# Fused cross-attention and FFN layer on one core: the attention's ACT, POOL and SP programs written out over all heads and rows instead of looped

## The chip, the cores and the metric

The kernel runs on one core of a Trainium2 chip. The metric is device time in microseconds (us), of which the median over several executions is given. The core has TensorE (PE), VectorE (DVE), ScalarE (ACT), GpSimd (POOL) and the DMA-issuing SyncE (SP), each with its own instruction stream; they meet only at semaphores.

## What is computed

A cross-attention layer followed by a feed-forward layer, over x of 4 x 512 tokens of width 512 (2048 rows) and a context of 4 x 1601 rows (6404 keys for every token, 16 heads of width 32). Cut to the attention:

```python
q = (x @ Wq + bq).reshape(1, B * N, H, hd)
kv = (cond @ Wkv + bkv).reshape(1, -1, 2, H, hd)
q = _fq_sym(q * scale, axis=-1); k = _fq_sym(k, axis=-1); v = _fq_sym(v, axis=2)
attn = einsum('bhqd,bhkd->bhqk', q, k)
attn = softmax(attn, axis=-1)
attn = _fq_unsigned(attn, axis=-1)      # round to 0..255 steps of the row's maximum
out = einsum('bhqk,bhkd->bhqd', attn, v)
x = x + out @ Wp + bp                   # then the FFN: LN, W1, gelu, W2, with block quantisation
```

## The kernel before

The program runs in phases, each ended by a barrier: weights of the FFN, queries, keys and values, the attention, and the rest (`finish`). The attention (lines 618 to 975) is the long one, from about 650 to 2590 us.

It works on 256 **rows**: a row is one head with one tile of 128 tokens; 16 token tiles (QT) make a head, and 16 heads follow each other. For a row:

- PE (`row_of_scores`, line 732) multiplies the tile's queries with all 6404 keys, in five chunks of about 1281 columns, into two alternating PSUM buffers `ps_s`.
- DVE (line 784) copies each chunk to the row buffer `s_row` in `arena` and takes its maximum; semaphore `scores_taken`.
- POOL joins the five maxima (lines 884, 891, 896) and makes the bias of the exponent (line 901); `bias_ready`.
- ACT (line 836) takes the exponent in two halves, which it writes as bytes (`n8`) and as int16 (`n16`), both in `arena`; `exp_done[0]` and `exp_done[1]`.
- SP transposes both halves by DMA: lines 711 (bytes, two to a word, into `words_T`) and 717 (into `nT`).
- POOL unpacks the bytes into `nT` (lines 909 and 910); `unpacked`.
- PE multiplies `nT` with the head's values (line 745) three rows later (LAG = 3), in four parts between the chunks of that later row, and ACT takes the output (line 842).

`s_row`, `nT` and the others hold two rows. So DVE can't write row n+2 before the exponent of row n has read `s_row`, and PE, whose program is in order, holds the next scores back when the values' part in front of them waits for `unpacked`. Within each head, ACT issues the loads for the next head: keys and queries (lines 808 and 810) at its token tiles 2 to 4, values (lines 815 to 820) at 5 to 7. POOL scales and rounds the next head's values (lines 922 and 930) at tiles 8 to 13.

How the programs are written: PE is looped in part, and has 16 written-out heads with a loop over the last 12 rows of each. DVE is written out over all 256 rows. ACT is written out for heads 0, 1, 14 and 15, and runs heads 2 to 13 in a loop whose body is two heads. POOL is written out for head 0, runs heads 1 to 14 in a loop of two heads with a loop over eight rows in each, and head 15 in a loop of two rows. SP runs all rows but the first two in a loop of two rows. In a loop the value that a wait compares with depends on the loop's counter, and is computed into a register. `settle` raises a semaphore that nobody waits for, by one, between two waits.

Of the kernel before, what the change touches and what calls it, by code (L numbers as in the profile page):

```python
# [42 lines left out]
def settle(eng, sem):  # L43


    eng.sem_inc(sem, 1)
# [573 lines left out]
def attention(nc, A, arena, q_dram, k_dram, v_dram, scales, v_scale, attn, zinv, wp, vectors, wp_loaded):  # L620

    T, K, C, H, HD = A.T, A.K, A.C, A.H, A.HD
    QT = T // P
# [4 lines left out]
    PAIRS = ROWS // 2  # L628
# [32 lines left out]
    VP = 3  # L661
# [3 lines left out]
    with Phase(nc, "a") as ph:  # L665
# [28 lines left out]
        sp_passed = ph.sem("sp_passed")  # L694
        pool_passed = ph.sem("pool_passed")
# [7 lines left out]
        @block.sync  # L703
        def _(sp):
            def turn(pair, u):
                row = pair * 2 + u
                after_first(sp, unpacked, row - 1)
                settle(sp, sp_passed)
                sp.wait_ge(exp_done[0], row + 1)
                settle(sp, sp_passed)  # L710
                sp.dma_start_transpose(words_T[:, u, :].rearrange("p (t q) -> p t q", q=P),
                                       n8[:, u, :].bitcast(U16)).then_inc(turned[u][0], 16)
                after_first(sp, values_done, row - 1)
                settle(sp, sp_passed)
                sp.wait_ge(exp_done[1], row + 1)
                settle(sp, sp_passed)
                sp.dma_start_transpose(nT[:, u, HALF_TILES:KT], n16[:, u, :].bitcast(FP16)).then_inc(turned[u][1], 16)

            turn(0, 0)
            turn(0, 1)  # L720
            with sp.Fori(1, PAIRS) as pair:
                for u in range(2):
                    turn(pair, u)

        @block.tensor
        def _(pe):
# [29 lines left out]

            PP = QT // 2

# [44 lines left out]
        def _(act):  # L803
# [41 lines left out]
            def rows_of_head(h, slot, last=False):  # L845
                for t in range(QT):
                    row = h * QT + t
                    exponent(row, t % 2)
                    if not (isinstance(row, int) and row < TAKE_LAG):
                        take_output(row - TAKE_LAG, t % 2)  # L850
                    if not last and 2 <= t < 8 and not (isinstance(h, int) and h == 0):
                        next_head(h + 1, 1 - slot, t - 2)
                    if isinstance(h, int) and h == 0 and t == 5:
                        act.wait_ge(v_rounded, VP)
                        for piece in range(3):
                            load_values(1, piece)
# [9 lines left out]
            for i, dram in enumerate((A.bp, A.ln_w, A.ln_b)):  # L866
                act.dma_start(vectors[:, i, :], dram.partition_broadcast(P)).then_inc(wp_loaded, 16)
            act.wait_ge(pad_done, 1)
            rows_of_head(0, 0)
            rows_of_head(1, 1)  # L870
            with act.Fori(1, H // 2 - 1) as hh:
                for slot in range(2):
                    rows_of_head(2 * hh + slot, slot)
            rows_of_head(H - 2, 0)
            rows_of_head(H - 1, 1, last=True)
            for row in range(ROWS - TAKE_LAG, ROWS):
                take_output(row, row % 2)

        @block.gpsimd
        def _(pool):  # L880
            def take_scales(row, u):
                after_first(pool, exp_done[1], row - 1)
                settle(pool, pool_passed)
                nc.gpsimd.tensor_copy(row_scale[:, u, :], scales[:, row % QT, row // QT, :]).then_inc(scale_ready, 1)

            def maximum(row, u):
                take_scales(row, u)
                m = row_max[:, u:u + 1]
                pool.wait_ge(scores_taken, row * NCH + 3)
                settle(pool, pool_passed)  # L890
                nc.gpsimd.tensor_scalar(m, part_max[:, u, 0:1], part_max[:, u, 1:2], part_max[:, u, 2:3],  # L891
                                        ALU.max, ALU.max).then_inc(three_done, 1)
                pool.wait_ge(scores_taken, row * NCH + NCH)
                pool.wait_ge(three_done, row + 1)
                settle(pool, pool_passed)
                nc.gpsimd.tensor_scalar(m, m, part_max[:, u, 3:4], part_max[:, u, 4:5],  # L896
                                        ALU.max, ALU.max).then_inc(row_max_ready, 1)
                pool.wait_ge(row_max_ready, row + 1)
                pool.wait_ge(scale_ready, row + 1)
                settle(pool, pool_passed)  # L900
                nc.gpsimd.tensor_scalar(bias[:, u:u + 1], row_max[:, u:u + 1], row_scale[:, u, 1:2], LN255,  # L901
                                        ALU.mult, ALU.add).then_inc(bias_ready, 1)

            def unpack(row, u):

                pool.wait_ge(turned[u][0], (row - u) * 8 + 16)
                after_first(pool, values_done, row - 1)
                settle(pool, pool_passed)
                nc.gpsimd.tensor_copy(low_T[u], bytes_T[:, u, :, 0])  # L909
                nc.gpsimd.tensor_copy(high_T[u], bytes_T[:, u, :, 1]).then_inc(unpacked, 1)  # L910

            def maximum_and_unpack(row, u):
                maximum(row, u)
                if not (isinstance(row, int) and row == 0):
                    unpack(row - 1, 1 - u)

            def scale_values(h, part):
                if part == 0:
                    pool.wait_ge(raw_loaded, h * 64 + 64)
                    settle(pool, pool_passed)  # L920
                tiles_of = v_raw[:, part * VT:(part + 1) * VT, :]
                nc.gpsimd.tensor_tensor(tiles_of, tiles_of, inv[:, ds(h * HD, HD)].unsqueeze(1).to_broadcast([P, VT, HD]),
                                        ALU.mult).then_inc(v_scaled, 1)

            def round_values(h, v_slot, part):
                pool.wait_ge(v_scaled, h * VP + (part + 1))
                if part == 0 and not (isinstance(h, int) and h < 2):
                    pool.wait_ge(values_done, (h - 1) * QT)
                settle(pool, pool_passed)
                nc.gpsimd.tensor_scalar(v_head[:, v_slot, part * VT:(part + 1) * VT, :],  # L930
                                        v_raw[:, part * VT:(part + 1) * VT, :], ROUND, ROUND,
                                        ALU.add, ALU.subtract).then_inc(v_rounded, 1)

            PP = QT // 2
            BEFORE = 4

            def rows_of_head(h, slot):

                with pool.Fori(0, BEFORE) as i:
                    for u in range(2):  # L940
                        maximum_and_unpack(h * QT + (2 * i + u), u)
                for part in range(VP):
                    maximum_and_unpack(h * QT + 2 * (BEFORE + part), 0)
                    scale_values(h + 1, part)
                    maximum_and_unpack(h * QT + 2 * (BEFORE + part) + 1, 1)
                    round_values(h + 1, 1 - slot, part)
                for i in range(BEFORE + VP, PP):
                    for u in range(2):
                        maximum_and_unpack(h * QT + (2 * i + u), u)

            def first_rows():
                for row in range(2 * BEFORE):
                    maximum_and_unpack(row, row % 2)
                for part in range(VP):
                    maximum_and_unpack(2 * (BEFORE + part), 0)
                    scale_values(1, part)
                    maximum_and_unpack(2 * (BEFORE + part) + 1, 1)
                    round_values(1, 1, part)
                for row in range(2 * (BEFORE + VP), QT):
                    maximum_and_unpack(row, row % 2)  # L960

            nc.gpsimd.partition_all_reduce(v_scale[:], v_scale[:], P, bass.bass_isa.ReduceOp.max).then_inc(reduced, 1)
            pool.wait_ge(inv_ready, 1)
            for part in range(VP):
                scale_values(0, part)
            for part in range(VP):
                round_values(0, 0, part)
            first_rows()
            with pool.Fori(0, H // 2 - 1) as hh:
                rows_of_head(2 * hh + 1, 1)  # L970
                rows_of_head(2 * hh + 2, 0)
            with pool.Fori((H - 1) * PP, H * PP) as pair:
                for u in range(2):
                    maximum_and_unpack(2 * pair + u, u)
            unpack(ROWS - 1, 1)


# [495 lines left out]
```

## Time and profile before

| | |
|---|---|
| median of 3 executions (lowest, highest) | 2925.6 us (2914.03, 2931.51) |
| the profiled execution: its time, its span | 2919.24 us, 2917.4 us |
| mean granted TensorE clock | 0.808 |
| busy PE, DVE, ACT, POOL | 78%, 86%, 68%, 48% of the span |
| first and last of the 1280 chunks on DVE | 662.9 and 2579.0 us |

The span runs from the first to the last instruction of one execution; the time of that execution has 1.8 us more around it. The profile gives the attention its share: 16 heads take 1917.5 us of the span, about two thirds.

### The profile page before, as it was taken

The page shows a single profiled execution, that of the slowest core. Times are in us where ns is not written, and L with a number is a line of the kernel's source. Part 1 is how long each engine was busy: PE and PEld are TensorE (multiplying, and loading weights), DVE is VectorE, ACT ScalarE, POOL GpSimd, SP SyncE. Part 2 cuts the span into 40 slices and gives each one's busy share as a digit, 9 for nine tenths or more (in the row PEclk, how much of TensorE's full clock was granted, in tenths as well). Part 3 has the DMA queues.
Part 4 walks back from the last instruction along what each step waited for, and adds up shares of the span by engine and source line. Part 5 has one row for each costly group of instructions (what it writes and reads, how often), then busy time and mean ns, then how long its engine had stood idle before and what let it go on. Part 6 is the DMA issues. An engine that isn't in the chain of part 4 may idle for free. (4 is left out here: it accounts for less than half of the span.)

```text
span 2917.4 us, 58686 instructions
## 1 busy us (share of the span) xinstructions
PE 2268.8 (78%) x20020; PEld 1192.2 (41%) x20020; DVE 2513.0 (86%) x3665; ACT 1993.3 (68%) x1859; POOL 1400.3 (48%) x1772
## 2 busy tenths in 40 slices
PE   0379999976778788888778777878877888767876
PEld 0234555532444444444344444444434444433333
DVE  8665666657999999999899999999989999957887
ACT  1113444435888888888788888888878788855554
POOL 0001111114666657667576575765756667653331
PEclk9699999985887777777776678777778677888989
DMA  6112323338999999999999999999999999980000
GB/s 239 67 27 99 110 97 126 108 106 159 168 212 177 194 197 176 204 188 189 188 174 194 166 197 200 176 202 190 181 187 173 192 197 182 180 219 4 15 15 26
DMA packets 1420697, 444.96 MB, mean 153 GB/s; under 512 B 1377512, under 2 KB 1392872, under 8 KB 1417872
## 3 DMA queue, kind: packets, MB, share of 16 engines
q1 hardware_dynamic: 1311664, 402.10, 68.0%
q10 hardware_dynamic: 108864, 40.92, 7.6%
q8 instruction: 67, 1.10, 0.2%
q14 instruction: 102, 0.84, 0.1%
HBM read 80.41 MB, written 43.77 MB: 43 GB/s over the span
## 5 line engine op out<-in xcount | busy, mean ns | idle before, releaser
L784 DVE TENSOR_SCALAR_CACHE_REDUCE arena<-a_ps_s 128x1281 f32<-128x1281 f32 (+1 forms) x1280 | 1828.6, 1489 | 87.3 <-PE a_ps_s L732 53.5
L836 ACT ACTIVATE arena<-arena,a_bias,a_row_scale 128x3328 uint8<-128x3328 f32 (+1 forms) x512 | 1560.0, 3048 | 301.3 <-POOL a_bias L901 264.2
L732 PE MATMUL a_ps_s<-arena,a_q_rep 96*128 96x512 bf16 (+2 forms) x3840 | 1239.4, 445 | 345.3 <-DVE arena L784 316.8
L745 PEld LDWEIGHTS a_ps_o<-a_v_head,a_nT 128*128 128x128 f16 x13056 | 526.7, 103 | 340.8 <-issue 184.3
L909 POOL CAST a_nT<-arena 128x1664 int16<-128x1664 uint8 x256 | 401.8, 1569 | 521.4 <-DMA arena<-arena 501.0
L732 PEld LDWEIGHTS a_ps_s<-arena,a_q_rep 96*128 (+1 forms) x3840 | 316.2, 110 | 788.4 <-DVE arena L784 433.2
L745 PE MATMUL a_ps_o<-a_v_head,a_nT 128*128 128x32 f16 x13056 | 519.6, 184 | 77.0 <-POOL a_nT L910 59.7
L910 POOL CAST a_nT<-arena 128x1664 int16<-128x1664 uint8 x256 | 402.8, 1573 | 0.0
L471 POOL TENSOR_TENSOR kv_parts<-kv_rest,kv_parts 128x512 bf16<-128x512 f32 (+1 forms) x51 | 59.0, 1156 | 578.9 <-ACT kv_parts L586 578.9
L591 ACT ACTIVATE kv_stage<-kv_ps_t 128x1024 bf16<-128x1024 bf16 (+1 forms) x51 | 51.4, 1007 | 204.8 <-PE kv_ps_t L508 204.8
L499 PE MATMUL kv_ps_k<-wkv,kv_ctxT 128*128 128x512 f32 (+1 forms) x408 | 185.3, 597 | 0.0
L499 PE MATMUL kv_ps_v<-wkv,kv_ctxT 128*128 128x512 f32 (+1 forms) x408 | 183.4, 592 | 0.0
L896 POOL TENSOR_SCALAR a_row_max<-a_row_max,a_part_max 128x1 f32<-128x1 f32 x256 | 92.1, 360 | 85.8 <-POOL a_row_max L891 42.4
L499 PEld LDWEIGHTS kv_ps_v<-wkv,kv_ctxT 128*128 128x128 f32 (+1 forms) x408 | 76.7, 188 | 98.4 <-issue 98.4
L559 DVE TENSOR_TENSOR kv_rest<-kv_kq,kv_parts 128x512 f32<-128x512 f32 (+1 forms) x51 | 35.3, 692 | 81.9 <-issue 81.9
L784 DVE DVE_READ_ACCUMULATOR arena<-a_ps_s 128x1 f32 x1280 | 105.6, 83 | 0.0
L499 PEld LDWEIGHTS kv_ps_k<-wkv,kv_ctxT 128*128 128x128 f32 (+1 forms) x408 | 73.4, 190 | 75.0 <-issue 74.9
L930 POOL TENSOR_SCALAR a_v_head<-a_v_raw 128x544 f16<-128x544 f32 x48 | 98.6, 2055 | 0.0
L836 ACT ACTIVATION_READ_ACCUMULATOR arena<-arena,a_bias,a_row_scale (+1 forms) x512 | 95.9, 187 | 0.0
L901 POOL TENSOR_SCALAR a_bias<-a_row_max,a_row_scale 128x1 f32<-128x1 f32 x256 | 66.6, 260 | 59.3 <-POOL a_row_max L896 58.6
L891 POOL TENSOR_SCALAR a_row_max<-a_part_max 128x1 f32<-128x1 f32 x256 | 93.2, 364 | 0.5
L369 PE MATMUL w_ps_t<-ident,arena 128*128 128x128 bf16 x128 | 12.3, 289 | 86.3 <-DVE arena L293 86.3
(157 smaller groups left out, 1946.5 us busy)
## 6 DMA issues: line engine op xcount, KB each, us to landing
arena<-k_parts_transposed ACTq DMA_DIRECT2D x48, 400.2 KB, 4.9
k_parts_transposed<-kv_stage SPq DMA_DIRECT2D x10, 1920.0 KB, 7.9
kv_ctx<-in_ctx_dram SPq DMA_DIRECT2D x10, 1280.0 KB
v<-arena SPq DMA_DIRECT2D x10, 1280.0 KB
arena<-in_L_ffn_W_dram SPq DMA_DIRECT2D x2, 4096.0 KB, 20.8
a_v_raw<-v ACTq DMA_DIRECT2D x32, 208.0 KB
a_q_rep<-q_transposed ACTq DMA_DIRECT2D x48, 128.0 KB, 5.8
a_v_raw<-v ACTq DMA_DIRECT2D x16, 384.0 KB
```

Of the source, the lines that this page charges most:

```text
L471: nc.gpsimd.tensor_tensor(parts[0:r, 2, :], rest1[0:r, :], parts[0:r, 1, :], ALU.subtract).then_inc(lo_ready, 1)
L499: last = nc.tensor.matmul(ps[0:r, u, :], ctxT[:, u, j, 0:r], wkv[:, j, col:col + C], start=(j == 0), stop=(j == CC - 1))
L732: last = nc.tensor.matmul(ps_s[:, b, n0:n0 + w], q, k_parts[0:3 * HD, slot, start[c] + n0:start[c] + n0 + w], start=True, stop=True)
L745: last = nc.tensor.matmul(ps_o[:, u, 0:HD], nT[:, u, j, :], v_head[:, v_slot, j, :], start=(j == 0), stop=(j == KT - 1))
L784: nc.vector.tensor_scalar(s_row[:, u, start[c]:start[c] + size[c]], ps_s[:, (u + c) % 2, 0:size[c]], 1.0, None, ALU.mult, ALU.max, accum_o ...
L836: nc.scalar.activation(out, s_row[:, u, keys_of_half[half]], ACT.Exp, scale=row_scale[:, u, 0:1], bias=bias[:, u:u + 1], accum_out=zsum[:, ...
L891: nc.gpsimd.tensor_scalar(m, part_max[:, u, 0:1], part_max[:, u, 1:2], part_max[:, u, 2:3], ALU.max, ALU.max).then_inc(three_done, 1)
L896: nc.gpsimd.tensor_scalar(m, m, part_max[:, u, 3:4], part_max[:, u, 4:5], ALU.max, ALU.max).then_inc(row_max_ready, 1)
L901: nc.gpsimd.tensor_scalar(bias[:, u:u + 1], row_max[:, u:u + 1], row_scale[:, u, 1:2], LN255, ALU.mult, ALU.add).then_inc(bias_ready, 1)
L909: nc.gpsimd.tensor_copy(low_T[u], bytes_T[:, u, :, 0])
L910: nc.gpsimd.tensor_copy(high_T[u], bytes_T[:, u, :, 1]).then_inc(unpacked, 1)
L930: nc.gpsimd.tensor_scalar(v_head[:, v_slot, part * VT:(part + 1) * VT, :], v_raw[:, part * VT:(part + 1) * VT, :], ROUND, ROUND, ALU.add, ...
```

## The change

Three programs of the attention are written out. SP's loop over pairs of rows, ACT's over pairs of heads, and POOL's three kinds of loop become Python loops, so that every wait compares with a constant and every address is one. All calls of `settle` in SP's and POOL's programs of the attention go. The order of the operations on each engine, their shapes, their semaphores and the points at which loads are issued stay as they were; PE's and DVE's programs, the other phases and the last phase are the same in both files.

```diff
@@ SP
             def turn(pair, u):
                 row = pair * 2 + u
                 after_first(sp, unpacked, row - 1)
-                settle(sp, sp_passed)
                 sp.wait_ge(exp_done[0], row + 1)
-                settle(sp, sp_passed)
                 sp.dma_start_transpose(words_T[:, u, :].rearrange("p (t q) -> p t q", q=P),
                                        n8[:, u, :].bitcast(U16)).then_inc(turned[u][0], 16)
                 after_first(sp, values_done, row - 1)
-                settle(sp, sp_passed)
                 sp.wait_ge(exp_done[1], row + 1)
-                settle(sp, sp_passed)
                 sp.dma_start_transpose(nT[:, u, HALF_TILES:KT], n16[:, u, :].bitcast(FP16)).then_inc(turned[u][1], 16)
-            turn(0, 0)
-            turn(0, 1)
-            with sp.Fori(1, PAIRS) as pair:
+            for pair in range(PAIRS):
                 for u in range(2):
                     turn(pair, u)
@@ ACT
-            rows_of_head(0, 0)
-            rows_of_head(1, 1)
-            with act.Fori(1, H // 2 - 1) as hh:
-                for slot in range(2):
-                    rows_of_head(2 * hh + slot, slot)
-            rows_of_head(H - 2, 0)
-            rows_of_head(H - 1, 1, last=True)
+            for h in range(H):
+                rows_of_head(h, h % 2, last=(h == H - 1))
@@ POOL: in maximum, take_scales, unpack, scale_values, round_values
                 pool.wait_ge(row_max_ready, row + 1)
                 pool.wait_ge(scale_ready, row + 1)
-                settle(pool, pool_passed)
...
-            def rows_of_head(h, slot):
-                with pool.Fori(0, BEFORE) as i:
-                    for u in range(2):
-                        maximum_and_unpack(h * QT + (2 * i + u), u)
-                for part in range(VP):
-                    maximum_and_unpack(h * QT + 2 * (BEFORE + part), 0)
-                    scale_values(h + 1, part)
-                    maximum_and_unpack(h * QT + 2 * (BEFORE + part) + 1, 1)
-                    round_values(h + 1, 1 - slot, part)
...
+            BEFORE = 8
+            def rows_of_head(h):
+                for t in range(QT):
+                    maximum_and_unpack(h * QT + t, t % 2)
+                    part = (t - BEFORE) // 2
+                    if h + 1 < H and 0 <= part < VP:
+                        if t % 2 == 0:
+                            scale_values(h + 1, part)
+                        else:
+                            round_values(h + 1, (h + 1) % 2, part)
...
-            first_rows()
-            with pool.Fori(0, H // 2 - 1) as hh:
-                rows_of_head(2 * hh + 1, 1)
-                rows_of_head(2 * hh + 2, 0)
-            with pool.Fori((H - 1) * PP, H * PP) as pair:
-                for u in range(2):
-                    maximum_and_unpack(2 * pair + u, u)
+            for h in range(H):
+                rows_of_head(h)
             unpack(ROWS - 1, 1)
```

What stands on the engines. First POOL, at a head's first row (before: the start of the loop over eight rows; `ISA` rows and `REGISTER_ALU` rows are handled by the engine's sequencer and serve the waits on registers and the addresses):

```order
L939 ISA
L884 ISA [waits a_second_exp_done]
L884 REGISTER_ALU
L884 COPY a_row_scale<-scales 128x2
L889 ISA
L891 TENSOR_SCALAR a_row_max<-a_part_max 128x1 [waits a_scores_taken]
L893 REGISTER_ALU
L894 REGISTER_ALU [waits a_scores_taken]
L896 TENSOR_SCALAR a_row_max<-a_row_max,a_part_max 128x1 [waits a_three_done]
L901 TENSOR_SCALAR a_bias<-a_row_max,a_row_scale 128x1 [waits a_row_max_ready,a_scale_ready]
L906 ISA
L909 CAST a_nT<-arena 128x1664 [waits a_odd_first_turned,a_values_done]
```


The same row in the changed kernel:

```order
L872 COPY a_row_scale<-scales 128x2 [waits a_second_exp_done]
L878 TENSOR_SCALAR a_row_max<-a_part_max 128x1 [waits a_scores_taken]
L882 TENSOR_SCALAR a_row_max<-a_row_max,a_part_max 128x1 [waits a_three_done,a_scores_taken]
L886 TENSOR_SCALAR a_bias<-a_row_max,a_row_scale 128x1 [waits a_scale_ready,a_row_max_ready]
L893 CAST a_nT<-arena 128x1664 [waits a_values_done,a_odd_first_turned]
L894 CAST a_nT<-arena 128x1664
```


Only the six operations of the row are left, with all their waits in themselves.

Next ACT, at an odd row whose second half is followed by the issue of keys and queries (before: in the loop, heads 2 to 13):

```order
L833 REGISTER_ALU
L836 ISA [waits a_odd_first_turned,a_bias_ready]
L836 ACTIVATE arena,a_zsum<-arena,a_bias,a_row_scale 128x3328
L836 ISA [waits a_odd_second_turned]
L836 ACTIVATE arena,a_zsum<-arena,a_bias,a_row_scale 128x3076
L842 ISA [waits a_values_done]
L842 ACTIVATE attn<-a_ps_o 128x32
L808 ISA
L808 DMA arena<-k_parts_transposed 32x6404
L810 DMA a_q_rep<-q_transposed 32x2048
```


The same in the changed kernel:

```order
L830 ACTIVATE arena,a_zsum<-arena,a_bias,a_row_scale 128x3328 [waits a_odd_first_turned,a_bias_ready]
L830 ACTIVATE arena,a_zsum<-arena,a_bias,a_row_scale 128x3076 [waits a_odd_second_turned]
L836 ACTIVATE attn<-a_ps_o 128x32 [waits a_values_done]
L802 DMA arena<-k_parts_transposed 32x6404
L804 DMA a_q_rep<-q_transposed 32x2048
```


Ten rows become five; the two exponents, the output's copy and the two loads follow each other as before.

Last SP, as a piece of the difference: the second row of its loop of two rows with the loop's end, and the start of the written-out program.

```order
-L709 REGISTER_ALU [waits a_unpacked]
-L711 DMA_TRANSPOSE arena<-arena 128x13x128 [waits a_first_exp_done]
-L717 DMA_TRANSPOSE a_nT<-arena 128x25x128 [waits a_values_done,a_second_exp_done]
-L721 REGISTER_ALU
-L721 COMPARE_AND_BRANCH
+L709 DMA_TRANSPOSE arena<-arena 128x13x128 [waits a_first_exp_done]
+L713 DMA_TRANSPOSE a_nT<-arena 128x25x128 [waits a_second_exp_done]
+L709 DMA_TRANSPOSE arena<-arena 128x13x128 [waits a_first_exp_done]
+L713 DMA_TRANSPOSE a_nT<-arena 128x25x128 [waits a_second_exp_done]
+L709 DMA_TRANSPOSE arena<-arena 128x13x128 [waits a_first_exp_done,a_unpacked]
+L713 DMA_TRANSPOSE a_nT<-arena 128x25x128 [waits a_second_exp_done,a_values_done]
```

Two transposes a row are left, with all their waits in themselves, 512 in all. In the attention, ACT's program has 934 instructions now (447 before, the loop's body once), POOL's 1636 (389) and SP's 513 (15).

## Rows read from the trace of the kernel before

**Rows 1.** The page: its first line, and the instruction queue of section 3.

```profile
span 2917.4 us, 58686 instructions
...
q14 instruction: 102, 0.84, 0.1%
```

**Rows 2.** Busy DVE in heads 1, 2, 10, 12, 13, 14 and 15.

```profile
core 0: us, DVE busy (x), PEclk, DMA share, GB/s
...
795.90:910.80 114.90, 114.02 (x161) 0.79 1.05 195
910.80:1029.60 118.80, 114.42 (x161) 0.77 1.04 189
...
1868.65:1985.52 116.87, 114.28 (x161) 0.76 1.03 192
...
2104.00:2228.20 124.20, 114.27 (x161) 0.76 1.05 181
2228.20:2350.40 122.20, 114.80 (x161) 0.71 1.03 184
2350.40:2466.47 116.07, 114.12 (x161) 0.78 1.05 194
2466.47:2580.40 113.93, 113.67 (x161) 0.85 0.96 177
```

**Rows 3.** Line 784 (DVE), whole run: what it sat idle for (us, times).

```profile
  PE a_ps_s L732: 53.5, 44
  ACT arena L836: 25.7, 8
```

**Rows 4.** Line 836 (ACT), heads 2 to 13: who waited for it (us, times).

```profile
  POOL a_row_scale L884: 19.5, 6
  DVE arena L784: 7.3, 6
```

**Rows 5.** Timeline, head 3, second row of the head.

```profile
1039.95 0.18 POOL L884 COPY a_row_scale<-scales 128x2 f32 x1 [3.16 <-issue]
...
1041.35 0.26 POOL L901 TENSOR_SCALAR a_bias<-a_row_max,a_row_scale 128x1 f32<-128x1 f32 x1 [0.23 <-POOL a_row_max L896]
...
1041.81 3.16 ACT L836 ACTIVATE arena<-arena,a_bias,a_row_scale 128x3328 uint8<-128x3328 f32 x1 [3.39 <-POOL a_bias L901]
...
1045.10 1.49 DVE L784 TENSOR_SCALAR_CACHE_REDUCE arena<-a_ps_s 128x1281 f32<-128x1281 f32 x1 [1.16 <-ACT arena L836]
```

**Rows 6.** Timeline, head 6, 30 to 51 us after its start.

```profile
1412.54 6.48 SPq L717 DMA_TRANSPOSE a_nT<-arena  x1
...
1419.27 3.87 SPq L711 DMA_TRANSPOSE arena<-arena  x1
...
1423.32 7.61 SPq L717 DMA_TRANSPOSE a_nT<-arena  x1
...
1430.33 1.57 POOL L909 CAST a_nT<-arena 128x1664 int16<-128x1664 uint8 x1 [7.09 <-DMA arena<-arena]
...
1430.69 1.49 DVE L784 TENSOR_SCALAR_CACHE_REDUCE arena<-a_ps_s 128x1280 f32<-128x1280 f32 x1 [4.21 <-PE a_ps_s L732]
...
1431.52 1.51 SPq L711 DMA_TRANSPOSE arena<-arena  x1
...
1433.22 6.20 SPq L717 DMA_TRANSPOSE a_nT<-arena  x1
```

**Rows 7.** Timeline, head 1, 37 us after its start.

```profile
833.31 5.24 SPq L717 DMA_TRANSPOSE a_nT<-arena  x1
...
833.81 0.26 POOL L901 TENSOR_SCALAR a_bias<-a_row_max,a_row_scale 128x1 f32<-128x1 f32 x1 [0.23 <-POOL a_row_max L896]
...
834.10 3.16 ACT L836 ACTIVATE arena<-arena,a_bias,a_row_scale 128x3328 uint8<-128x3328 f32 x1 [1.59 <-POOL a_bias L901]
```

**Rows 8.** Line 711 (SP), first transpose (ns min/median/max), whole run.

```profile
L711 SPq DMA_TRANSPOSE arena<-arena x256: 1469/1490/6982, 691.9 to 2585.0; - x128
```

**Rows 9.** Line 717 (SP), second transpose, likewise.

```profile
L717 SPq DMA_TRANSPOSE a_nT<-arena x256: 3689/3909/8812, 694.9 to 2588.0; - x128
```

More of the change, by code:

```diff
@@ L894, in maximum @@
                 pool.wait_ge(three_done, row + 1)
-                settle(pool, pool_passed)
                 nc.gpsimd.tensor_scalar(m, m, part_max[:, u, 3:4], part_max[:, u, 4:5],
@@ L899, in maximum @@
                 pool.wait_ge(scale_ready, row + 1)
-                settle(pool, pool_passed)
                 nc.gpsimd.tensor_scalar(bias[:, u:u + 1], row_max[:, u:u + 1], row_scale[:, u, 1:2], LN255,
@@ L907, in unpack @@
                 after_first(pool, values_done, row - 1)
-                settle(pool, pool_passed)
                 nc.gpsimd.tensor_copy(low_T[u], bytes_T[:, u, :, 0])
@@ L919, in scale_values @@
                     pool.wait_ge(raw_loaded, h * 64 + 64)
-                    settle(pool, pool_passed)
                 tiles_of = v_raw[:, part * VT:(part + 1) * VT, :]
@@ L928, in round_values @@
                     pool.wait_ge(values_done, (h - 1) * QT)
-                settle(pool, pool_passed)
                 nc.gpsimd.tensor_scalar(v_head[:, v_slot, part * VT:(part + 1) * VT, :],
@@ L932, in round_values @@
                                         ALU.add, ALU.subtract).then_inc(v_rounded, 1)
-            PP = QT // 2
-            BEFORE = 4
-            def rows_of_head(h, slot):
-                with pool.Fori(0, BEFORE) as i:
-                    for u in range(2):
-                        maximum_and_unpack(h * QT + (2 * i + u), u)
-                for part in range(VP):
-                    maximum_and_unpack(h * QT + 2 * (BEFORE + part), 0)
-                    scale_values(h + 1, part)
-                    maximum_and_unpack(h * QT + 2 * (BEFORE + part) + 1, 1)
-                    round_values(h + 1, 1 - slot, part)
-                for i in range(BEFORE + VP, PP):
-                    for u in range(2):
[L949 to L960, printed above, removed]
+            BEFORE = 8
[8 more added lines that the diff above has]
+                            round_values(h + 1, (h + 1) % 2, part)
             nc.gpsimd.partition_all_reduce(v_scale[:], v_scale[:], P, bass.bass_isa.ReduceOp.max).then_inc(reduced, 1)
@@ L967, in _ @@
                 round_values(0, 0, part)
-            first_rows()
-            with pool.Fori(0, H // 2 - 1) as hh:
-                rows_of_head(2 * hh + 1, 1)
-                rows_of_head(2 * hh + 2, 0)
-            with pool.Fori((H - 1) * PP, H * PP) as pair:
-                for u in range(2):
-                    maximum_and_unpack(2 * pair + u, u)
+            for h in range(H):
+                rows_of_head(h)
             unpack(ROWS - 1, 1)
```

1 line of the change is left out of this document (removed).

## The prediction

> **What bounds the kernel now.** I read first how long each head takes on DVE, then what DVE waits for, then the places of these waits on the timeline.
>
> The last head takes 113.93 us, of which DVE is busy 113.67 [rows 2]: DVE's 80 copies a head, one every 1.42 us, are the floor of the attention. The heads before take more: head 1 114.90 and head 14 116.07, but heads 2 to 13 together 2350.40 - 910.80 = 1439.6, or 119.97 each, the shortest 116.87 and the longest 124.20, while DVE's busy time stays at 114.3 to 114.8 [rows 2]. So DVE loses 6 us a head, as waits and not as slower work. It waits for PE's scores 53.5 us in 44 places and for ACT's exponent 25.7 us in 8 [rows 3].
>
> Of the waits for ACT, 7.3 us in 6 places lie in heads 2 to 13 [rows 4]. One is shown: POOL jumps back to the start of its loop of two heads, its first operation of the row comes 3.16 us late for nothing that the profile names ("issue"), the bias and the exponent come late behind it, and DVE stops 1.16 us, since it may not overwrite the row buffer [rows 5]. This repeats 6 times, 19.5 us on POOL in all, or 3.25 each [rows 4].
>
> The waits for PE are the larger part and have another cause: SP. Unloaded, its two transposes take the queue 1.49 and 3.91 us (medians) [rows 8, 9], with gaps of a few tenths under 6 us of the 7.1 us that DVE needs for a row. While the next head's keys, queries and values are loaded, they take longer: 6.48, 3.87, 7.61 and 6.20 us [rows 6]. Two of them then exceed a row's time, SP runs late, POOL waits 7.09 us for the bytes, PE's values wait for POOL, and the scores queued behind them on PE come 4.21 us late at DVE [rows 6].
>
> **What the change takes away.** Three things.
>
> First, the jumps of POOL's outer loop. The DVE loss of 7.3 us [rows 4] should go in full; nothing takes POOL's place, since ACT is then ready earlier too.
>
> Second, the sequencer's work on registers. On ACT it shows between the bias and the exponent: in a looped head the bias ends at 1041.35 + 0.26 = 1041.61 and the exponent starts at 1041.81, 0.20 us later [rows 5]; in head 1, where ACT is written out, 833.81 + 0.26 = 834.07 and 834.10, 0.03 us later [rows 7]. On SP it shows where the queue is the late one: the first transpose of an even row follows the last of the row before by 1431.52 - (1423.32 + 7.61) = 0.59 us, that of an odd row by 1419.27 - (1412.54 + 6.48) = 0.25, and the second transpose follows the first by 1433.22 - (1431.52 + 1.51) = 0.19 [rows 6]. I take 0.19 for all gaps that are left: 0.40 + 0.06 = 0.46 us of the queue saved in every two rows. For the `settle` calls as such I count nothing beyond it.
>
> Third, reloads of code. The looped programs of POOL and ACT are fetched anew in each pass, by DMA: 102 fetches of 0.84 MB in all for the run, 8.2 KB each, in the one queue [rows 1]. Written out they pass once. These fetches fall into the same DMA engines as the transposes.
>
> **The sum.** The trace holds a trial of ACT's part: heads 1 and 14 have ACT written out and the full loads of a next head, but POOL and SP in loops. They take 114.90 and 116.07, mean 115.5, and both are shorter than the shortest of the twelve looped heads [rows 2]. In chance order that would happen once in 91 (two of fourteen). I take 115.5 for heads 2 to 13: 1439.6 - 12 x 115.5 = 53.6 us. That includes the 7.3 us of POOL's jumps, of which head 1 and head 14 have none inside.
>
> SP's 0.46 us in two rows makes 1.4 us over the six rows with loads. Heads 1 and 14 lose 115.5 - 113.9 = 1.6 us each against the last head, so up to that much can still be had; I take 0.5, a third of the queue's 1.4, since lateness of SP reaches DVE only beyond its slack of two rows: 14 x 0.5 = 7.0 us, bounds 0 and 14 x 1.6 = 22.4.
>
> Nothing is counted for head 0, whose ACT is written out already, nor for PE, DVE and the other phases. The work per row stays as it was, hidden under DVE's 7.1 us: if DVE were no cover, SP's queue would be next, with 1.49 + 3.91 + 2 x 0.19 = 5.8 us a row [rows 8, 9].
>
> New costs: the written-out streams must be fetched too. DVE bounds that: its program is written out over 1280 copies already, and all its idle time ends with PE or ACT, none with issue [rows 3]. I take 0; the other end stands under the rivals.
>
> Sum against the profiled execution (span 2917.4 and 1.8 around it, 2919.2): 2919.2 - 53.6 - 7.0 = 2858.6. The median of the runs shown is 6.4 above the profiled one. If the runs differ by their stops, a part of this goes as well; I add half, 3, and forecast 2862 us.
>
> A rule of the skill is weighed here. The back edge of POOL costs 3.25 us [rows 4] and that of SP 0.59 - 0.19 = 0.40 [rows 6]. The Trainium skill, Advanced Engine Details and Errata, Control Flow Timing, has a compare-and-branch at about 108 ns. By that figure, an estimate, six back edges would cost 0.6 us and written-out code would bring next to nothing; the trace's rows are 30 and 4 times as large, so they decide.
>
> **Rivals.**
>
> A: the loads alone make the stops. That heads 1 and 14 are short would be luck, and the transposes of heads 2 to 13 stay stretched to 6 or 7 us by the loads [rows 6], which the change leaves as they are. Then only POOL's jumps go: 2919.2 - 7.3 = 2912, with the 3 from the median 2915. For it: in head 1 the second transpose is stretched too, to 5.24 us [rows 7]. Against it: the order of the heads' lengths. Chance 0.16; half of it with enough of SP's gain to come below 2911.
>
> B: the code arrives late, and the kernel is slower. SP had 15 instructions and stayed in its loop; now it has 513, and POOL 1636. If a stream that runs on stops at the border of a block as POOL does at its jump, each stop costs 3.25 us on its engine [rows 4], and on SP in the loaded rows it reaches DVE in full. Two stops a head make 32 x 3.25 = 104, so 2862 + 104 = 2966. It decides against the change from 63 / 3.25 = 19 stops passed on in full. Against it: DVE's program, without one. Chance 0.06.
> The Trainium skill, Runtime: NRT & Kernel Launch, Instruction fetch mechanics, says that the sequencer fetches the next block during the current one, so that a crossing is mostly hidden, and that a taken branch out of the window is not. That DVE has no issue stop and POOL's jump has one agrees.
>
> C: PE becomes the bound. With fewer stops PE works more densely, and the granted clock falls; it was 0.75 to 0.79 in most heads, but 0.85 in the last [rows 2], which speaks against it. If it fell to where DVE's busy time is 114.8 instead of 114.1 a head (heads 13 and 14) [rows 2], as scores come some tenths late, and again as much is lost in waits, the price is 16 x 0.7 x 2 = 22 us: 2884. Chance 0.07.
>
> **How the numbers follow.** The forecast, 2862, has 0.71. Its own range is from all of SP's gain, 2919.2 - 53.6 - 22.4 = 2843, to heads 2 to 13 at 117.5 instead of 115.5, 24 us more, 2886. With A's half and C the range is 2843 to 2911, which leaves out B, A's other half and a tail of 0.04, 0.18 in all. A measurement of this kernel can tell about 0.5% from no change, that is 2911 to 2940. Faster: 0.70 + 0.07 + 0.08 = 0.85; within: A's other half and the last 0.01 of the forecast, 0.09; slower: 0.06.
>
> **What would show it.** Right, if the stretch of a head on DVE is 114 to 116 us in all heads but the first; if bias to exponent is 0.03 us everywhere; if no POOL operation waits 3 us for issue; if the gap from one row's last transpose to the next row's first is 0.19 or less; and if the instruction queue has far fewer than 102 fetches. Wrong, if rows 3 to 6 of the heads still show DVE stops of 2 to 4 us behind PE with transposes of 6 us (then A), or issue waits on SP, POOL or ACT at new places (B), or many DVE gaps of 0.1 us at a low clock (C).

## The result, and the profile after

The changed kernel takes 2878.2 us (median of 4 executions, 2873.8 to 2891.2) against 2927.15 for the kernel before in the same comparison: ratio 0.985, 95% interval 0.980 to 0.989. The forecast was 2862, range 2843 to 2911. The profiled execution has a span of 2877.7 us. The highest time of the changed kernel, 2891.2, lies below the lowest of the one before, 2914.0. (One execution in all the comparisons, one of POOL alone with 3067.8 us at a granted clock of 0.667, was slowed as a whole and is left out of the times below.)

DVE busy in the stretch of each head, of the changed kernel; the columns are those of [rows 2]:

```profile
core 0: us, DVE busy (x), PEclk, DMA share, GB/s
660.33:783.78 123.45, 114.10 (x160) 0.72 0.94 180
783.78:898.77 114.99, 114.29 (x163) 0.76 1.04 196
898.77:1015.25 116.48, 114.27 (x161) 0.81 1.06 191
...
1131.17:1253.38 122.21, 114.37 (x159) 0.74 1.05 183
1253.38:1376.07 122.69, 114.13 (x161) 0.79 1.05 184
1376.07:1497.41 121.34, 114.15 (x163) 0.76 1.05 185
1497.41:1611.99 114.58, 114.17 (x161) 0.79 1.07 195
...
2309.23:2427.81 118.58, 114.37 (x163) 0.74 1.04 188
2427.81:2541.99 114.18, 113.92 (x162) 0.82 0.97 178
sum 1881.66, DVE 1826.69; mean DVE 114.17
```

Where the 39.7 us between the two spans went: the first chunk of the attention comes 2.6 us earlier (660.33 against 662.9), head 0 takes 123.45 us instead of 795.9 - 662.9 = 133.0, heads 2 to 13 take 2309.23 - 898.77 = 1410.5 instead of 1439.6, heads 1 and 14 together 233.6 instead of 231.0 [rows 2]. That is 2.6 + 9.6 + 29.1 - 2.6 = 38.7, and the rest, 1.0, lies in the last head and behind the attention. The floor of about 114 us has not moved. Heads 4, 5 and 6 still take 121 to 123, the others behind head 0 take 114 to 119.

The waits of DVE behind head 0, first of the changed kernel, then of the one before; the columns are total us, times, longest:

```profile
DVE arena L778 <- PE a_ps_s L726: 39.6, 24, 5.9
```

```profile
DVE arena L784 <- PE a_ps_s L732: 53.5, 44, 4.2
DVE arena L784 <- ACT arena L836: 7.3, 6, 1.6
```

The waits for ACT, which came from POOL's jumps, are gone. Those for PE are fewer and longer. One of them on the timeline of the changed kernel, head 4, 36 to 56 us after its start:

```profile
1166.85 9.96 SPq L713 DMA_TRANSPOSE a_nT<-arena  x1
...
1176.90 7.68 SPq L709 DMA_TRANSPOSE arena<-arena  x1
1178.52 0.26 POOL L886 TENSOR_SCALAR a_bias<-a_row_max,a_row_scale 128x1 f32<-128x1 f32 x1
1178.81 3.16 ACT L830 ACTIVATE arena<-arena,a_bias,a_row_scale 128x3328 uint8<-128x3328 f32 x1 [4.87 <-POOL a_bias L886]
...
1184.67 3.82 SPq L713 DMA_TRANSPOSE a_nT<-arena  x1
...
1186.71 1.57 POOL L893 CAST a_nT<-arena 128x1664 int16<-128x1664 uint8 x1 [7.94 <-DMA arena<-arena]
1186.95 1.49 DVE L778 TENSOR_SCALAR_CACHE_REDUCE arena<-a_ps_s 128x1280 f32<-128x1280 f32 x1 [4.77 <-PE a_ps_s L726]
```

This is the picture of [rows 6] again: two transposes of 9.96 and 7.68 us in a row, POOL waits 7.94 for the bytes, DVE stops 4.77. It is the sign that the prediction named for its rival A. What the change touches is seen in the gaps: 1176.90 - (1166.85 + 9.96) = 0.09 us from a row's last transpose to the next row's first, where it was 0.59 or 0.25, and 1178.81 - (1178.52 + 0.26) = 0.03 us from bias to exponent, where it was 0.20 [rows 5, 6].

The page's line on the instruction queue:

```profile
q14 instruction: 76, 0.62, 0.1%
```

102 fetches have become 76 [rows 1].

### The profile page after: what moved, and what is told of

It is laid out like the page before. It is cut to its first block and busy times, and to the rows that moved or that the text cites. A ratio compares the mean times of both kernels' runs of the same rounds, so it can differ in the third digit from the quotient of the medians.

```text
span 2877.7 us, 54224 instructions
## 1 busy us (share of the span) xinstructions
PE 2229.9 (77%) x20003; PEld 1186.4 (41%) x20020; DVE 2509.7 (87%) x3665; ACT 1995.9 (69%) x1859; POOL 1403.9 (49%) x1772
## 5 line engine op out<-in xcount | busy, mean ns | idle before, releaser
L778 DVE TENSOR_SCALAR_CACHE_REDUCE arena<-a_ps_s 128x1281 f32<-128x1281 f32 (+1 forms) x1280 | 1825.4, 1489 | 55.0 <-PE a_ps_s L726 39.6
L726 PE MATMUL a_ps_s<-arena,a_q_rep 96*128 96x512 bf16 (+2 forms) x3840 | 1207.9, 436 | 359.3 <-DVE arena L778 325.1
L559 DVE TENSOR_TENSOR kv_rest<-kv_kq,kv_parts 128x512 f32<-128x512 f32 (+1 forms) x51 | 35.3, 692 | 81.9 <-issue 81.9
L830 ACT ACTIVATION_READ_ACCUMULATOR arena<-arena,a_bias,a_row_scale 128x1 f32 x512 | 95.7, 187 | 0.0
L1141 PE MATMUL f_ps_y<-arena 128*128 128x512 bf16 x242 | 67.0, 438 | 15.0 <-ACT arena L1221 14.3
```

The costliest lines, as they stand in the source:

```text
L726: last = nc.tensor.matmul(ps_s[:, b, n0:n0 + w], q, k_parts[0:3 * HD, slot, start[c] + n0:start[c] + n0 + w], start=True, stop=True)
L778: nc.vector.tensor_scalar(s_row[:, u, start[c]:start[c] + size[c]], ps_s[:, (u + c) % 2, 0:size[c]], 1.0, None, ALU.mult, ALU.max, accum_o ...
L830: nc.scalar.activation(out, s_row[:, u, keys_of_half[half]], ACT.Exp, scale=row_scale[:, u, 0:1], bias=bias[:, u:u + 1], accum_out=zsum[:, ...
L1141: last = nc.tensor.matmul(ps_y[:], gT[:, t % 2, j, :], w2[:, j, :], start=False, stop=(j == FC - 1))
```

## The experiments

Each kernel's time was taken beside the kernel before on the same chip, and ratios are to that. There were four such comparisons, in which the kernel before took 2927.15 us (changed), 2925.3 (each engine alone, wait split off), 2920.0 (ACT and POOL, settle on SP, keys cut) and 2916.75 (loads spread or in halves), so between comparisons the ratios say more than the times. "Heads 2 to 13" is the time in the profiled execution from the first DVE chunk of head 2 to that of head 14, "PE waits" what DVE waited for PE behind head 0. These three columns are of one execution each, which can lie off the median: that of "ACT and POOL, SP as before" is the fastest of its kernel, 14 us below the median, that of "SP alone" lies 8 us below, that of "changed, loads spread" 8 us above.

| kernel | median us | ratio (95%) | head 0 | heads 2 to 13 | PE waits |
|---|---|---|---|---|---|
| before | 2927.15 | 1 | 133.0 | 1439.6 | 53.5 |
| changed | 2878.2 | 0.985 (0.980 to 0.989) | 123.5 | 1410.5 | 39.6 |
| ACT alone | 2902.4 | 0.993 (0.991 to 0.995) | 131.9 | 1414.8 | 35.2 |
| SP alone | 2939.8 | 1.007 (1.004 to 1.010) | 132.6 | 1449.4 | 67.2 |
| POOL alone | 2891.0 | 0.989 (0.986 to 0.991) | 123.6 | 1416.6 | 38.6 |
| changed, wait split off | 2883.5 | 0.987 (0.984 to 0.990) | 132.8 | 1398.0 | 26.9 |
| ACT and POOL, SP as before | 2882.4 | 0.987 (0.984 to 0.989) | 123.5 | 1396.1 | 24.7 |
| changed, settle on SP | 2882.3 | 0.987 (0.984 to 0.990) | 123.7 | 1402.3 | 35.3 |
| changed, keys cut | 2838.9 | 0.972 (0.969 to 0.976) | 123.5 | 1371.4 | 0 |
| before, keys cut | 2866.1 | 0.982 (0.978 to 0.985) | 132.8 | 1387.9 | 1.2 |
| changed, loads spread | 2897.0 | 0.990 (0.987 to 0.994) | 123.1 | 1422.7 | 46.7 |
| before, loads spread | 2951.2 | 1.009 (1.006 to 1.013) | 132.7 | 1463.7 | 62.5 |
| ACT and POOL, loads spread | 2902.2 | 0.994 (0.991 to 0.997) | 123.4 | 1421.2 | 41.9 |
| changed, keys in halves | 2850.8 | 0.976 (0.972 to 0.979) | 123.6 | 1384.3 | 5.4 |

### Each engine alone

The three parts of the diff, each put into the kernel before by itself. ACT alone:

```diff
-            with act.Fori(1, H // 2 - 1) as hh:
-                for slot in range(2):
-                    rows_of_head(2 * hh + slot, slot)
...
+            for h in range(H):
+                rows_of_head(h, h % 2, last=(h == H - 1))
```

> The kernel before with ACT alone written out; POOL and SP keep loops and settle. The forecast's reading (heads 1 and 14 are short because ACT is written out there): heads 2 to 13 fall from 1439.6 us to near 12 x 115.5 = 1386, at least by 25 us, head 0 stays at 133, total about 2885 to 2900. Rival (ACT's registers cost only slack, the gain comes from SP and POOL): heads 2 to 13 within 10 us of 1440, total 2915 to 2928, though bias to exponent falls from 0.20 to 0.03 us in both.

Measured: 2902.4 us, 23 below the kernel before in that comparison (2925.3), heads 2 to 13 at 1414.8, 24.8 us shorter. The expectation asked for at least 25 and a total of at most 2900, so both are just missed. Against the 53.6 that the forecast read off heads 1 and 14, less the 7.3 of POOL's jumps, which this kernel still has, it is half. The forecast's reading holds in its direction, and the rival, no gain from ACT, is out.

What of ACT's loop costs the time isn't separated by this run. Bias to exponent fell from 0.20 to 0.04 us, but ACT's jumps back went too, which the prediction didn't look at. In the kernel before, from ACT's branch at the end of its loop to its next instruction pass 2.5 to 3.9 us at each of the 5 jumps. Most of it is hidden under the exponent that still runs, and 0.9 to 1.1 us show at four of them, as at the first row of head 4:

```profile
1157.91 3.16 ACT L836 ACTIVATE arena<-arena,a_bias,a_row_scale 128x3328 uint8<-128x3328 f32 x1 [0.90 <-issue]
```

SP alone:

```diff
-                settle(sp, sp_passed)
...
-            with sp.Fori(1, PAIRS) as pair:
+            for pair in range(PAIRS):
```

> The kernel before with SP alone written out and its settle calls gone. If SP's queue is what makes the stops behind PE, 0.40 us and more saved in each two rows shortens heads 2 to 13 by 10 to 30 us (total 2895 to 2917). By the forecast's sum SP was worth 7 us, total near 2920. In both the gap from the last transpose of a row to the first of the next falls from 0.59 and 0.25 to about 0.09 us. Head 0 stays at 133 us.

Measured: 2939.8 us, 0.7% slower than before. Neither reading expected that. The queue's gaps fell as expected, but the waits for PE rose from 53.5 to 67.2 us. Heads 5, 7, 9, 11 and 13 take 123 to 127 us, the even ones 117 to 119. The odd ones are those that begin with POOL's jump, which this kernel still has. Why it costs more there than in the kernel before is not settled.

POOL alone:

```diff
-                settle(pool, pool_passed)
...
-            with pool.Fori(0, H // 2 - 1) as hh:
-                rows_of_head(2 * hh + 1, 1)
-                rows_of_head(2 * hh + 2, 0)
+            for h in range(H):
+                rows_of_head(h)
```

> The kernel before with POOL alone written out, its settle calls gone. Forecast's reading: the issue waits of 3 us vanish and with them 7.3 us. New theory on head 0: its 9.6 us come from POOL, whose configuration for the broadcast multiply no longer stands behind the wait for the loaded values: head 0 falls to about 123 us here, and in no kernel in which POOL is as before. Total 2927 - 10 - 7 = about 2910; if the shorter chain from DVE's last chunk to the bias (0.88 to 0.57 us) feeds the stops behind PE too, 2890 to 2905.

Measured: 2891.0 us, 34 below. Head 0 is at 123.6, as the theory on it says, and heads 2 to 13 at 1416.6, 23 shorter, of which POOL's jumps are 6.9 (DVE's waits for ACT fell from 7.3 to 0.4). The last figure of the expectation, 2890 to 2905, is met, and the waits for PE fell from 53.5 to 38.6. That the shorter chain to the bias is what did this was the expectation's reason; the run doesn't separate it from the jumps and the `settle` calls.

The parts make 23 - 14 + 34 = 43 us, the whole change 49 in its own comparison: they add up roughly. ACT and POOL together should then be better than the changed kernel:

> ACT and POOL written out as in the changed kernel, SP's loop and settle calls as before. If the parts add up as measured alone (SP alone cost 0.7%), this is the faster version: 2878 - 14 = about 2864 us. Rival (what SP written out costs beside looped ACT and POOL, it does not cost beside written-out ones, since it shares the reloads of code with them): the same as the changed kernel or slower by SP's longer gaps, 2878 to 2885 us.

Measured: 2882.4, ratio 0.987 as for the changed kernel at 0.985. What SP alone costs, it doesn't cost once ACT and POOL are written out, and it gains nothing there either. The reason that the expectation's rival names, shared reloads of code, is not shown by this. The fetches in the page's instruction queue (102 before, 84 with ACT alone, 86 with POOL alone, 110 with SP alone, 76 changed, 68 here) don't follow the times closely: 68 and 76 stand beside 2882.4 and 2878.2 us. The same for SP's `settle` calls put back in the changed kernel:

```diff
+                settle(sp, sp_passed)
                 sp.wait_ge(exp_done[0], row + 1)
+                settle(sp, sp_passed)
                 sp.dma_start_transpose(words_T[:, u, :].rearrange("p (t q) -> p t q", q=P),
```

> The changed kernel with SP's four settle calls a row put back, written out. The gaps of SP's queue grow from 0.09 and 0.17 to about 0.2 us and no code is looped. If issuing the transposes earlier is what costs in the SP-alone kernel, this is faster than the changed one, by up to 14 us (2864). If a free queue helps, it is slower by some us (2880 to 2888). If the settle calls only cost slack, 2878 within 5.

Measured: 2882.3, 4 us above the changed kernel and with an interval that covers it. It lies in the range of two of the three readings, a little slower (2880 to 2888) and slack alone (2878 within 5), so only the first is out: issuing the transposes earlier is not what costs here.

### Head 0

POOL's first multiply by `inv` is preceded by a configuration of the engine. In the kernel before:

```profile
L922 POOL TENSOR_TENSOR a_v_raw<-a_v_raw,a_inv x48: 1317/1338/1347, 675.7 to 2451.5; 128x544 f32<-128x544 f32 x48
...
L922 POOLq MODIFY_POOL_CONFIG  x2: 11/11/11, 664.9 to 664.9; - x2
```

and in the changed one:

```profile
L905 POOL TENSOR_TENSOR a_v_raw<-a_v_raw,a_inv x48: 1321/1341/1348, 663.8 to 2412.9; 128x544 f32<-128x544 f32 x48
L905 POOLq MODIFY_POOL_CONFIG  x2: 98/98/98, 656.5 to 656.5; - x2
```

The configuration is issued at 656.5 instead of 664.9, and the multiply starts 663.8 - 656.5 = 7.3 us behind it, where it was 10.8. By the semaphore events in the traces the last of the values lands at 662.6 in the changed kernel and at 664.7 in the one before. The theory: before, the wait for the loaded values stood in an instruction of its own (a `settle` followed it), ahead of the configuration. Now the wait is part of the multiply, and the configuration runs while the values still load: the multiply starts 1.2 us behind their landing, where it was 11.1. So up to 6.1 of the 7.3 us can be the wait for the values, and the 7.3 us are no measure of the configuration alone. The test puts one `settle` back:

```diff
                 if part == 0:
                     pool.wait_ge(raw_loaded, h * 64 + 64)
+                    settle(pool, pool_passed)
```

> The changed kernel with one edit: a settle call back behind the wait for the loaded values, so that this wait stands in an instruction of its own again. Theory: POOL's configuration falls behind the wait again, head 0 goes from 123.4 back to about 133 us, all else as in the changed kernel: about 2878 + 10 = 2888. Rival (head 0 was shorter by chance, or by the earlier code fetch): no difference beyond noise, 2878, and head 0 at 123.

In its profile:

```profile
L906 POOL TENSOR_TENSOR a_v_raw<-a_v_raw,a_inv x48: 1319/1342/1348, 674.6 to 2408.3; 128x544 f32<-128x544 f32 x48
L906 POOLq MODIFY_POOL_CONFIG  x2: 11/11/11, 663.7 to 663.7; - x2
```

The configuration is at 663.7 again, the multiply at 674.6, and head 0 takes 132.8 us. The theory stands. The total rose by 5 us only (2883.5 against 2878.2), less than the 9.4 of head 0 and within both intervals. In the profiled execution heads 2 to 13 were 12 us shorter than those of the changed kernel (1398.0 against 1410.5), with nothing else in them than one `settle` a head. The four executions of the changed kernel alone differ by 17 us, so a difference of 12 us between two single executions is scatter as far as can be told.

### What makes the stops behind PE

The keys' load of each next head is cut from 6404 to 64 columns, from head 2 on, in the changed kernel and in the one before. This leaves out nearly all of that load.

```diff
-                act.dma_start(k_parts[s * HD:(s + 1) * HD, slot, :],
-                             k_dram[s, ds(h * HD, HD), :]).then_inc(head_loaded[slot], 16)
+                cols = K if isinstance(h, int) and h < 2 else 64
+                act.dma_start(k_parts[s * HD:(s + 1) * HD, slot, 0:cols],
+                             k_dram[s, ds(h * HD, HD), 0:cols]).then_inc(head_loaded[slot], 16)
```

> The changed kernel with the load of a head's keys cut from 6404 columns to 64 from head 2 on (this leaves out nearly all of the keys' load; the output is then that of old keys). If the stops behind PE come from the loads stretching the transposes, heads 2 to 14 fall to 114 to 115 us each: total about 2878 - 25 = 2853. Rival (the values' loads with their small rows, or PE's own code fetches, make the stops): they stay at the same tiles, total above 2868.

> The kernel before with the same cut of the keys' load. If loops and settle cost time only through the loads' stops, it comes down to within the head-0 difference and POOL's jumps of the changed kernel's version: 2853 + 10 + 7 = about 2870. If the loops cost time by themselves in every row, it stays 30 us or more above it.

(In the kernel before, as in the changed one, the cut holds from head 2 on; where the head is a loop counter it is always cut.) Heads 2 to 13 in one stretch, of the changed kernel with keys cut, then of the kernel before with keys cut:

```profile
898.57:2269.95 1371.38, 1366.97 (x1921) 0.82 1.02 186
```

```profile
909.03:2296.88 1387.85, 1371.03 (x1921) 0.78 1.00 184
```

With the keys cut, the changed kernel's 12 heads take 114.3 us each, the floor, with no wait for PE or ACT at all. No transpose takes over 6 us any more, where 18 of 512 did in the changed kernel. The second one in this profile:

```profile
L713 SPq DMA_TRANSPOSE a_nT<-arena x256: 3691/3798/4843, 683.6 to 2505.7; - x128
...
DMA to landing us min/median/max: 5.6/5.9/8.8
```

So the stops that are left in it come from the keys' loads; the values' loads and PE's code alone make none. The total, 2838.9, was lower than expected. The kernel before comes to 2866.1, near the 2870 expected, but it was expected 17 us above the other and is 27, made up of head 0 (132.8 - 123.5 = 9.3), 9.6 us of waits for ACT, nearly all at POOL's jumps, and some 7 more in heads 2 to 13. Its even heads from 4 to 12 take 114.3 to 115.0 us, though bias to exponent is 0.20 us there and SP's gaps are as before: where nothing else is late, the registers, the `settle` calls and ACT's jumps cost nothing. DVE's waits for PE are 1.2 us in all, so SP's gaps make no stops by themselves either.

With full loads, the whole change brings 49 us by its own comparison, and 38 by those of the two kernels that differ from it only on SP. So 11 to 22 us more than 27 appear only with loops and full loads together, and the intervals leave room for a few us less or more. That a stretched transpose costs more where the row is late already would explain it, but no run isolates this.

### The loads moved

In the changed kernel the loads of keys and queries go from token tiles 2, 3, 4 to 2, 9, 12:

```diff
-                    if not last and 2 <= t < 8 and not (isinstance(h, int) and h == 0):
-                        next_head(h + 1, 1 - slot, t - 2)
+                    step = {2: 0, 4: 3, 5: 4, 6: 5, 9: 1, 12: 2}.get(t)
+                    if not last and step is not None and not (isinstance(h, int) and h == 0):
+                        next_head(h + 1, 1 - slot, step)
```

> The changed kernel with the three loads of keys and queries of the next head moved apart, from token tiles 2, 3, 4 to 2, 9, 12, and the values' from 5, 6, 7 to 4, 5, 6. If the stops come from several loads in consecutive rows, SP recovers in between and most of the 25 to 40 us of stops go: 2845 to 2860. Rival (each load makes its own stop): about 2878, with the stops moved to rows 3 to 4, 10 and 13.

Measured: 2897.0, ratio 0.990 (0.987 to 0.994) where the changed kernel had 0.985 (0.980 to 0.989): no better, and worse if anything. The larger stops behind PE are now at rows 5, 12 and 15 of a head, counted from 0, and at row 0 of the next DVE waits 0.5 to 1.1 us for ACT. The rival was right in kind, each load makes its own stop, some three rows behind its issue; its time, 2878, was too low. The two others with the same spread:

> The kernel before with the loads spread the same way. It tells whether the change's gain hangs on the bunched loads: with keys cut, before and changed were 27 us apart, and 43 us with the loads. If the spread removes the collisions, 2866 to 2885, 25 to 30 us above the spread changed kernel.

Measured: 2951.2, 1% slower than before, clear of its interval (1.006 to 1.013). The two spread kernels are 54 us apart, against 49 with the loads as they were, so the change's gain doesn't hang on the loads standing together. Behind head 0 DVE waits 62.5 us for PE and 23.9 for ACT, against 46.7 and 7.4 in the spread changed kernel. The expected numbers were too low by 66 us and more, as they rested on the spread taking collisions away.

> ACT and POOL written out, SP looped with settle, loads spread. If SP's own writing out is worth nothing once ACT and POOL are written out, it is equal to the spread kernel within 5 us.

Measured: 2902.2, 5 us above the spread changed kernel: SP's part is worth nothing that can be told here either. Against ACT and POOL with the loads as they were (0.987, 0.984 to 0.989) its ratio, 0.994 (0.991 to 0.997), is clearly worse, which shows for the third time that moving whole loads apart doesn't help.

Last, each load of keys as two of 3202 columns, one row apart:

```diff
+            def load(h, slot, s, halves=((0, K // 2), (K // 2, K))):
+                for lo, hi in halves:
+                    act.dma_start(k_parts[s * HD:(s + 1) * HD, slot, lo:hi],
+                                  k_dram[s, ds(h * HD, HD), lo:hi]).then_inc(head_loaded[slot], 16)
...
+                    step = {2: 0, 3: 6, 4: 3, 5: 4, 6: 5, 8: 1, 9: 7, 11: 2, 12: 8}.get(t)
```

> As the spread kernel, and each load of keys in two halves of 3202 columns a row apart (tiles 2, 3, 8, 9, 11, 12). If what stretches a transpose is the size of a load in one row, this is as good or better than the spread one: 2840 to 2855. If it is the number of loads that counts, it is slower than the spread one.

Measured: 2850.8 us, ratio 0.976 (0.972 to 0.979) against the kernel before, clear of the changed kernel's interval. This is the fastest of the kernels with the whole computation. The second transpose in its profile, under it the same of the changed kernel, and last of the spread one:

```profile
L713 SPq DMA_TRANSPOSE a_nT<-arena x256: 3676/4204/6311, 684.6 to 2521.8; - x128
...
DMA to landing us min/median/max: 5.6/6.2/9.8
```

```profile
L713 SPq DMA_TRANSPOSE a_nT<-arena x256: 3697/3832/9965, 682.8 to 2549.2; - x128
...
DMA to landing us min/median/max: 5.6/5.9/18.4
```

```profile
L713 SPq DMA_TRANSPOSE a_nT<-arena x256: 3695/4242/8776, 684.9 to 2569.2; - x128
...
DMA to landing us min/median/max: 5.6/6.2/10.8
```

The longest time in the queue falls from 9.97 us to 6.31, while the median rises a little. Of both transposes together 18 take over 6 us in the changed kernel, 21 in the spread one and 2 with halves. DVE's waits for PE fall from 39.6 to 5.4 us. The same bytes move at nearly the same places in the spread kernel, in whole loads, at 2897.0 us in the same comparison. So it is the size of one load, not the load of a head as a whole, that makes the stops. The time to landing tells them apart less well: its maximum is 18.4 us in the changed kernel and 9.8 with halves, but 10.8 in the spread kernel, with 46.7 us of stops.

## Why the prediction was right, and where it was off

The time lies in the range and the direction was forecast. The size was not: between the profiled executions the sum had 53.6 + 7.0 = 60.6 us, and 39.7 were measured; between the medians it is 49. And a part of that is luck. Only 29.1 - 2.6 = 26.5 of the 39.7 us lie in heads 1 to 14, to which the sum's terms belong; 9.6 come from head 0, for which it had nothing, and 2.6 from an earlier start of the attention, which nothing here explains. Without the 9.6 of head 0 the time would be about 2888, still in the range that is widened for the rivals, but outside the forecast's own, 2843 to 2886. By its own steps:

- **POOL's jumps**, 7.3 us: right. No operation of POOL waits for issue behind head 0, and no DVE wait for ACT is left there.
- **Heads 2 to 13 at the length of heads 1 and 14**, 53.6 us with the jumps: the direction was right, the size was not: 29.1 in the profiled execution of the changed kernel, and 37.3, 41.6 and 43.5 in the three that differ from it only in one `settle` a head or on SP (1402.3, 1398.0 and 1396.1; the last is of the fastest execution of its kernel). The step that failed is the trial of two heads. They were short in that execution by more than their form gives: the changed kernel's heads 1 to 14, all of that form, run from 114.6 to 122.7 us. The trial also put all on ACT; alone it brings 24.8, and POOL alone 23.
- **SP's queue**, 7 us: wrong. Its gaps fell even further than assumed (0.09), but the time did not follow. Alone it costs 0.7%; beside written-out ACT and POOL it is worth nothing measurable. The step took a few tenths of lateness of the queue for a part of the stops. With the keys cut, the kernel before has the old gaps and 1.2 us of waits for PE, and with halves, where the gaps are those of the changed kernel and the long transposes are gone, the waits fall to 5.4.
- **Head 0**, taken as 0 us: wrong by 9.6. This made up for a part of the missing rest. The step overlooked that a wait's place decides what is issued in front of it.
- **New costs of code** (rival B), 0: right. POOL has no wait for issue behind head 0, and the 24.4 us that ACT's exponent waits for issue there, in 8 places, lie behind ACT's own issue of the values' loads. Before it was 21.9 in 10, of which four, 4.0 us together, were ACT's jumps. The fetches went down, though only from 102 to 76, which isn't the "far fewer" of the prediction's signs.
- **Rival C**: did not come. The mean granted clock rose from 0.808 to 0.826, and DVE's busy time in a head stayed at 113.9 to 114.4.
- **Rival A** (the loads alone make the stops), chance 0.16, had a right half: without the keys' loads there is no stop behind PE at all. By the prediction's own signs more speaks for it than the range shows: 8 of the 15 heads behind the first take over 116 us, where 114 to 116 was the sign of being right, and stops of up to 5.9 us behind PE are left in rows 6 and 7, counted from 0, with transposes of over 6 us. But it took the loops as innocent, and they are not.

What stays open is why SP alone makes the looped kernel slower, why the same load makes a stop of 6 us in one head and none in another, and which part of writing out ACT and POOL (registers, `settle` calls, jumps, fetches) makes the stops behind PE smaller: no run takes one of these away by itself.

## What to carry to other kernels

When a pipeline stops now and then, ask first for the longest single transfer that shares the DMA engines with it: halving it brought 28 us here, and moving it brought nothing or made things worse. Writing the loops out paid most beside such a transfer (38 to 49 us, against 27 without it); measure each engine's part, since here one of the three brought nothing. A wait that stands in an instruction of its own holds back everything that the compiler puts behind it, here a configuration, for 9.4 us of head 0, and a wait in the consumer does not. And two short stretches of one trace are no trial where the stretches scatter by as much as they differ.

## What the runs showed of the hardware

- From POOL's configuration to its first multiply pass 10.9 us when it is issued at 663.7, behind the landing of the values, and 7.3 us when it is issued early (656.5 to 663.8), of which the first 6.1 are also the wait for these values. The Trainium skill, GPSIMD Engine Reference, 2.1 Instruction dispatch, gives about 6 us for the first call of newly loaded code, without the wait for its operands. The 10.9 us, which hold no such wait, are above it; the 7.3 us can't decide, as the profile calls them issue and doesn't take the wait off. Why the late one is longer is open.
- A jump back on POOL leaves it idle for 3.25 us on average [rows 4]; from the branch to its sequencer's next instruction it is 4.4 to 6.2 us at the six. On ACT it is 2.5 to 3.9 us at five, of which 0.9 to 1.1 show as idle time at four. On SP it is about 0.4 (0.59 with the jump and `settle`, 0.18 written out with `settle`).
- A load of keys of 400 KB beside the transposes takes single ones of them to 9.97 us, where the longest is 4.84 without these loads and 6.31 with each load in two halves.
- Heads 2 to 13 of two kernels that differ there in one `settle` a head took 1410.5 and 1398.0 us, and four executions of the changed kernel 2873.8 to 2891.2: two stretches of single executions tell no difference of 12 us in 1400.
